# A hybrid Mamba, experts and attention kernel: the Mamba stage's B products as eight transposes, and the order of its engines laid out anew

## The reference, cut to what matters

```python
xz = hidden @ in_proj_w.T;  x, z = halves of xz          # 512 + 512 channels
u = silu(causal_conv(x, width 4) + conv_b)
dt_lo, B, C = split(u @ x_proj_w.T)                      # 64, 16, 16 columns
delta = softplus(dt_lo @ dt_proj_w.T + dt_proj_b)
A = -exp(A_log)                                          # 512 x 16
h[t] = exp(delta[t] * A) * h[t-1] + (delta[t] * u[t]) * B[t]   # per channel and state
y[t] = sum over states of h[t] * C[t]
out = ((y + u * D) * silu(z)) @ out_proj_w.T
```

## Time and profile before

| what | value |
| --- | --- |
| median of 3 runs | 3267.97 us (3264.76 to 3269.45) |
| the profiled execution: its own time | 3268.12 us |
| its span in the trace | 3266.3 us |
| share of the span busy: PE, DVE, POOL, ACT | 83%, 70%, 65%, 52% |
| first scan of the Mamba stage | starts at 58.85 us |
| last product with C of the Mamba stage | starts at 1763.12 us |
| mean granted clock of TensorE | 0.909 of full |

### The profile page before, as it was taken

The page is one execution under the profiler, slowest core; times in us unless marked ns, Lnnn a source line. Parts: engine busy times, 40 slices in busy tenths (PEclk is TensorE's granted clock), DMA queues, the critical chain, the costliest instruction groups (busy, mean ns, idle before and its releaser), DMA issues.

```text
span 3266.3 us, 55217 instructions
## 1 busy us (share of the span) xinstructions
PE 2720.5 (83%) x20862; PEld 1519.8 (47%) x20862; DVE 2293.8 (70%) x2418; ACT 1706.3 (52%) x3090; POOL 2120.7 (65%) x1317
## 2 busy tenths in 40 slices
PE   7788778887888778887855599996999999469998
PEld 3233333333344334333333355564677777445565
DVE  3999999999999999999997522212667676542211
ACT  4677777777777777777762122222444443122222
POOL 2999999999999999999995044443333333034453
PEclk9899999988999889988976599998999999679999
DMA  5556655665566565665562033432111111213442
GB/s 145 122 124 144 149 137 124 145 152 137 141 135 149 144 140 126 143 149 139 129 139 76 16 71 81 90 59 57 40 54 47 54 47 41 69 41 80 90 91 26
DMA packets 227558, 330.13 MB, mean 101 GB/s; under 512 B 40705, under 2 KB 116993, under 8 KB 227170
## 3 DMA queue, kind: packets, MB, share of 16 engines
q1 hardware_dynamic: 202722, 292.51, 36.1%
q0 software_dynamic: 24576, 34.10, 6.2%
HBM read 240.53 MB, written 85.98 MB: 100 GB/s over the span
## 4 chain that ended last, share of the span: by engine, by line
PE 44%; POOL 25%; DVE 19%; issue 6%; ACT 2%; DMA 2%; SPq 0%; DVEq 0%; POOLq 0%; ACTq 0%
POOL m_side L649 15%; PE t_wb L2230 8%; POOL m_hc L658 7%; DVE m_pair L740 7%; PE f_h L1499 7%; PE g_h L1499 7%; DVE m_hc L740 5%; PE f_yp L1513 3%; PE g_yp L1513 3%; DVE m_hc L749 2%; PE t_num L2230 2%; PE t_a_ps L2230 2%; PE m_wk L870 2%; PE m_y L967 2%; PE m_pair L1025 2%
## 5 line engine op out<-in xcount | busy, mean ns | idle before, releaser
L649 POOL TENSOR_TENSOR m_side<-m_du_r,m_bc 128x1024 f32<-128x1024 f32 x416 | 974.7, 2368 | 10.0 <-DMA m_du_r<-ddd 10.0
L394 ACT ACTIVATE m_pair<-m_delta_r,m_a_neg 128x512 f32<-128x512 f32 x832 | 539.8, 681 | 188.7 <-DVE m_hc L749 129.1
L658 POOL TENSOR_TENSOR m_hc<-m_hc,m_bc 128x1024 f32<-128x1024 f32 x208 | 492.1, 2369 | 101.7 <-DVE m_hc L740 100.0
L740 DVE TENSOR_TENSOR_SCAN m_pair<-m_pair,m_side 128x1024 f32<-128x1024 f32 x240 | 548.1, 2284 | 4.7 <-POOL m_side L649 2.5
L967 PE MATMUL m_y<-m_hc,m_fold 128*32 128x512 f32 x2048 | 320.7, 700 | 226.9 <-DVE m_hc L749 118.8
L740 DVE TENSOR_TENSOR_SCAN m_hc<-m_pair,m_side 128x1024 f32<-128x1024 f32 x176 | 397.8, 2275 | 9.8 <-ACT m_pair L394 5.6
L749 DVE TENSOR_TENSOR m_hc<-m_pair,m_bc 128x1024 f32<-128x1024 f32 x304 | 370.5, 1219 | 7.4
L870 PE MATMUL m_wk<-m_xnT,m_w_in 128*128 128x512 f32 x488 | 262.9, 665 | 0.0
L870 PE MATMUL m_wk<-m_xs,m_cw_diag 128*128 128x512 f32 x480 | 229.3, 605 | 12.8 <-ACT m_xs L461 12.8
L1025 PE MATMUL m_pair<-m_b_diag,m_du_t 128*32 128x128 f32 x6144 | 203.9, 289 | 41.2 <-DVE m_hc L740 24.2
L1025 PEld LDWEIGHTS m_pair<-m_b_diag,m_du_t 128*32 128x32 f32 x6144 | 179.0, 117 | 122.0 <-issue 120.6
(11 more groups left out here) (339 smaller groups left out, 4881.4 us busy)
## 6 DMA issues: line engine op xcount, KB each, us to landing
m_delta_r<-ddd SPq DMA_DIRECT2D x252, 256.0 KB, 6.8
m_du_r<-ddd SPq DMA_DIRECT2D x252, 256.0 KB, 7.6
m_bc<-bcd SPq DMA_DIRECT2D x256, 128.0 KB, 2.9
ddd<-m_delta SPq DMA_DIRECT2D x31, 512.0 KB, 3.1
ddd<-m_du SPq DMA_DIRECT2D x31, 512.0 KB, 4.2
f_w<-in_w SPq DMA_DIRECT2D x24, 512.0 KB, 6.0
g_w<-in_w SPq DMA_DIRECT2D x24, 512.0 KB, 6.0
m_xt<-in_x SPq DMA_DIRECT2D x16, 512.0 KB, 10.5
```

What stands on the lines that cost most here:

```text
L394: last = nc.scalar.activation(to, delta_r[:, c % 2, q, :], ACT.Exp, scale=a_neg[:, c * NQ + q, st:st + 1])
L649: nc.gpsimd.tensor_tensor(side[:, un % RING, :, :], du_r[:, c % 2, 2 * h:2 * h + 2, :], bc[:, 0, st:st + 1, :].to_broadcast([P, 2, T]), AL ...
L658: nc.gpsimd.tensor_tensor(hc[:, un % RING, :, :], hc[:, un % RING, :, :], bc[:, 1, st:st + 1, :].to_broadcast([P, 2, T]), ALU.mult).then_i ...
L740: nc.vector.tensor_tensor_scan(to, decay, added, 0.0, ALU.mult, ALU.add).then_inc(S["scan"], 1)
```

## The change

The constants (`ORDER` gives for each chunk the (set of states, half) of its eight units; before they went in the order 0, 0, 1, 1, 2, 2, 3, 3):

```diff
-ON_POOL = (0, 3, 4, 8, 9, 12, 13, 16, 18, 21, 24, 27, 28)
-ON_PE = (2, 15, 18, 22, 27, 31)
-PE_SETS = (1, 3)
+BY_PE = 3
+ORDER = (((0, 0), (0, 1), (1, 0), (1, 1), (3, 0), (2, 1), (2, 0), (3, 1)),
+         ((0, 0), (0, 1), (2, 0), (1, 1), (1, 0), (3, 1), (3, 0), (2, 1)),
+         ((0, 0), (0, 1), (1, 0), (1, 1), (2, 0), (2, 1), (3, 0), (3, 1)),
+         ((0, 0), (0, 1), (3, 0), (3, 1), (1, 0), (1, 1), (2, 0), (2, 1)))
+SET = [st for units in ORDER for st, _ in units]
+ON_POOL = (0, 2, 4, 5, 8, 9, 11, 13, 18, 20, 22, 24, 26, 28)
+ON_PE = tuple(un for un in range(UN) if SET[un] == BY_PE)
```

So `ON_PE` is now (4, 7, 13, 14, 22, 23, 26, 27): eight units, all of set 3. ACT no longer makes diagonals. It makes the product itself, on transposed data (time on the partitions, where B is one value for each partition), and PE transposes it back:

```diff
-            def diag(b, i, n):
+            def scaled(b, g, n):
...
                 for k in range(TJ):
-                    last = nc.scalar.activation(b_diag[:, i, n, k, :], ident[:], ACT.Identity,
-                                                scale=b_t[:, k, PE_SETS[i] * NL + n:PE_SETS[i] * NL + n + 1])
+                    last = nc.scalar.activation(prod[:, :, :, k, n * SB:(n + 1) * SB],
+                                                du_t[:, k, :, :].rearrange("p c (h f d) -> p (c h) f d", h=2, d=SB),
+                                                ACT.Identity, scale=b_t[:, b % 2, k, BY_PE * NL + n:BY_PE * NL + n + 1])
...
             def b_products(b, un):
...
                 for f in range(2):
-                    q = 2 * h + f
                     for k in range(TJ):
-                        for n in range(NL):
-                            last = nc.tensor.matmul(pair[n * SB:(n + 1) * SB, un % 2, f * T + k * P:f * T + (k + 1) * P],
-                                                    du_t[:, c % 2, k, q * SB:(q + 1) * SB], b_diag[:, i, n, k, :],
-                                                    start=True, stop=True, skip_group_check=True)
+                        last = nc.tensor.transpose(pair[:, un % 2, f * T + k * P:f * T + (k + 1) * P],
+                                                   prod[:, c % 2 * 2 + h, f, k, :], ident[:])
```

More of the change, by code:

```diff
@@ L55 @@
 NE_, NG_ = E_BEFORE[UN], G_BEFORE[UN]
[L56 removed]
+E_FIRST = [min(un for un in ON_PE if un // 16 == g) for g in range(2)]
+E_LAST = [E_BEFORE[16], NE_]
 G_FIRST = [min(un for un in range(8 * c, 8 * c + 8) if un not in ON_PE) for c in range(4)]
[L58 removed]
+LAST_OF = [1 + max(un for un in range(UN) if SET[un] == st) for st in range(NSET)]
+A_IX = (0, 2, 4, 5)
+A_CONV = (3, 5, 7, 10)
+A_DUT = (29, 30, 7, 12)
+A_SILU = 11
+A_XD = 12
+A_BT = 14
+A_SOFT = (13, 15, 16, 17)
+A_Z = (19, 20, 22, 27)
+A_SCALE = ((31, 32, 33, 36), (14, 18, 18, 20))
+A_NORM_OUT = (23, 24)
+A_NORM_IN = (22, 24)
+A_PT = (28, 28)
+A_SCORE = 28
+A_TR = (29, 29)
+T_IX = (0, 1, 2, 4)
+T_CONV = ((0, 0), (3, 3), (4, 5), (7, 8))
+T_DUT = (30, 30, 5, 12)
+T_OUT = (7, 10)
+T_XP = (10, 12)
+T_BT = 13
+T_DT = (12, 14, 16, 17)
+T_Z = (18, 20, 21, 25)
+T_PT = 27
+T_TR = 28
+V_GATE = (11, 17, 31, 35)
+V_RES = (9, 11)
+V_SUM_OUT = (10, 11)
+V_SUM_IN = (10, 11, 12)
+V_DELTA = (14, 15, 16, 18)
+G_OUT = 14
+G_IN = 17
+G_DU = (18, 21)
 RESET = 1e30
@@ L192, in mamba @@
                  "ab ex sp de du dz ld_c ld_l ld_p st_p pd pz xn_h "
-                 "btr b_t dut du_t dg0 dg1 dA dBu dBp scan hD hP sum yg op x1 bs1 agg1 ve1 rstd1 nm1 xn1 pt ptev scm scev").split()
+                 "btr b_t dut du_t pr dA dBu dBp scan hD hP sum yg op x1 bs1 agg1 ve1 rstd1 nm1 xn1 pt ptev scm scev").split()
         S = {n: s.sem(n) for n in names}
@@ L583, in body @@
                         nc.scalar.preload_act_table_set("natural_log_exp_and_others")
-                    if post and un in (20, 22):
-                        out_norm3(b - 1, (20, 22).index(un))
+                    if post and un in A_NORM_OUT:
+                        out_norm3(b - 1, A_NORM_OUT.index(un))
+                    if prep and un == A_XD:
+                        xd_out(b + 1)
+                    if un == A_DUT[3]:
+                        dut_out(b, 3)
+                    for n in range(NL):
+                        if un == A_SCALE[1][n]:
+                            scaled(b, 1, n)
@@ new lines, in body @@
+                        if un in A_Z:
+                            iz_out(b + 1, 1 - par, A_Z.index(un))
+                    if ahead(b) and un in A_NORM_IN:
+                        in_norm2(b + 2, A_NORM_IN.index(un))
+                    for k in range(KC):
+                        if post and un == A_PT[k]:
+                            pt_out(b - 1, k)
+                    if post and un == A_SCORE:
+                        sc_out(b - 1)
+                    for k in range(KC):
+                        if ahead(b) and un == A_TR[k]:
+                            tr_out(b + 2, k)
@@ L615, in epilogue @@
+                    for c in range(2):
+                        if prep and un == A_DUT[c]:
+                            dut_out(b + 1, c)
+                    for n in range(NL):
+                        if prep and un == A_SCALE[0][n]:
+                            scaled(b + 1, 0, n)
             def epilogue():
@@ L825, in body @@
                     scan(b, un)
-                    gates = (13, 20, 31) if prep else (13, 20, 28)
+                    if post and un + UN == V_GATE[3]:
+                        gate(b - 1, 1 - par, 3)
+                    gates = V_GATE[:3] if prep else (V_GATE[0], V_GATE[1], 28)
                     if un in gates:
@@ new lines, in body @@
+                        for dt in range(KD):
+                            for half in range(2):
+                                if un == T_CONV[dt][half]:
+                                    conv(b + 1, dt, half)
+                    if un == T_DUT[2]:
+                        dut(b, 2, post, prep)
+                    if post and un in T_OUT:
+                        outp(b - 1, T_OUT.index(un), prep)
+                    if prep and un in T_XP:
+                        xp(b + 1, 1 - par, T_XP.index(un))
@@ L1176, in body @@
+                    if post and un == T_PT:
+                        ptr(b - 1, 0, prep)
+                        ptr(b - 1, 1, prep)
+                        gate_scores(b - 1)
+                    if ahead(b) and un == T_TR:
                         tr(b + 2, 0)
                         tr(b + 2, 1)
-                    if prep and un == 29:
-                        dut(b + 1, 0, post, ahead(b))
-                        dut(b + 1, 1, post, ahead(b))
+                    for c in range(2):
+                        if prep and un == T_DUT[c]:
+                            dut(b + 1, c, post, ahead(b))
```

180 lines of the change are left out of this document (68 added, 112 removed).

## The result

| | kernel before | changed kernel |
| --- | --- | --- |
| median on the same chip | 3266.42 us (4 runs, 3264.76 to 3269.45) | 3246.3 us (4 runs, 3244.88 to 3246.65) |
| ratio of the changed kernel | | 0.9938, interval 0.9926 to 0.995 |
| span of the profiled run | 3266.3 us | 3244.8 us |
| first scan, last product with C (start) | 58.85, 1763.12 us | 59.22, 1741.55 us |

The changed kernel is faster by 20 us, 32.5 were forecast. All of the gain lies in the Mamba stage: the last product with C starts 21.6 us earlier and the span is 21.5 us shorter.

What follows compares the result with a forecast made beforehand. DVE was taken to set the pace, 97% busy. Its work (-20.0 us), fewer waits over batches 1 to 14 (-10.5) and the last batch (-2) sum to -32.5 us: 3236 us from 3268.1, range 3208 to 3280.

Steps and rivals of the forecast that it cites:

- DVE's work: On DVE, products with C go from 19 to 18 units: 1.25 us less in each of 16 batches, 20.0 us.
- PE's new price: On PE, eight transposes for a PE unit's B product take 1.1 us, where the product took 1.95.
- ACT's new price: On ACT, a `scaled` instruction of 256 columns steps 0.40 us, so a call of `scaled` takes 1.6 us.
- The waits that go: DVE's waits before `mk_delta`, at unit 2's decay and the second residual, 2.55 us a batch, should go.
- The new waits: DVE waits 1.3 us at unit 4 and 0.5 for places a walk misses, 1.8 us a batch.
- the walk: Step-by-step schedule up to unit 4: scan 4 could start at 11.8 us, PE's transposes end at 12.6, 0.8 late.
- Rival (c): PE at half clock before unit 4: scan 4 waits 4.2 to 6 us; 3282 us in all, chance 0.18.
- The sign that it named: On PE, a clock near 0.5 in the first ten microseconds of a batch would show the forecast wrong.
- the rule that speaks for (c): On PE, the Trainium skill says transposes do not count as busy for the clock; the time would be 3282 us.
- Rival (b): One wait for another: DVE's new waits sum to 3.4 to 4.3 us a batch; 3262 to 3274 us, chance 0.10.
- First and last batch: At the ends: 0 within -4 and +4 us in the first batch, -2 in the last from shorter PE products.
- the likeliest case: Whole kernel: the prediction's own forecast, 3215 to 3256 us, was given a chance of 0.60.

Runs made afterwards that it cites:

- The experiment on the B products: The changed kernel with the eight transposes of each PE unit issued as plain matmuls against the identity; measured 1.0205 of the kernel before.

## Why the prediction was right or wrong

**DVE's work: right.** The forecast was 1.25 us a batch for the product, and the run with unit 20 on DVE shows that price (3.46 for 2.20 us). Busy time fell by 1.67, though. A part of the rest is that a gate between a scan and its own product costs little: scan, gate and product take 3.91 us of the pace (801.29 to 805.20), scan and product alone 3.46 (803.43 to 806.89 in the earlier trace rows), so the gate costs 0.45 for a duration of 0.67. One more of the four gates stands there than before. This part was only read off the rows; no run isolates it. DVE's statistics of the input moved too, from units 13 to 15 to 10 to 12, which the list of places leaves out.

**PE's new price, ACT's new price: right.** Eight transposes take 1.04 us (1.1 taken), four `scaled` 1.69 us (1.6) in steps of 0.40. POOL's and ACT's sums hold as well: 771.70 / 8 = 96.5 us a batch (96.4 forecast) and 655.64 / 8 = 82.0 (82). The Trainium skill, ScalarE: Activation LUTs, What ACT_TABLE_LOAD costs, gives 186 ns and 0.833 ns a column, and about 93 ns for each operand that is one value a partition. An estimate by that page is 492 ns for 256 columns; the trace, with 496, agrees.

**The waits that go: right.** `mk_delta`, the second residual and unit 2 have none left.

**The new waits: this step failed, while the time held.** The forecast put 1.3 us at unit 4 and 0.5 for all the rest, 1.8 us a batch. Measured are 2.24 at unit 4 (31.4 us in 14 batches) and 1.07 at unit 19.

- At unit 4 the place, the order of PE's tasks and their prices were right: from `d_term`'s end to the end of the transposes the walk had 7.35 us, the trace has 7.49 (811.07 to 818.56), and scan 4 was wanted at 11.8 us and could have started at 11.82. What was mis-sized is the head of the chain: `d_term` ends at 5.9 us and not 5.2 in the best batches, and a `total` and an `ix` at the low clock make the wait a microsecond longer in 8 batches of 14. The prediction left 0.5 us for the clock.
- Rival (c) named this mechanism but costed it at 3.4 to 5 us, for a `conv` and an `ix` at the low clock. In the changed kernel only the `total` and the first `ix` behind the idle time are slow; the `conv` follows it after 0.68 us and runs in 3.70. The sign that it named, a clock near 0.5 in the first ten microseconds of a batch, didn't come: the second row of the stretches has 1.00, and the low clock lies ahead of the batch. The experiment on the B products agrees with the rule that speaks for (c), without isolating it. The time of (c), 3282, was not reached: at unit 4 the clock is worth the mean of 2.24 less the 1.42 of full clock (from the kernel with small transposes as matmuls), 0.8 us a batch, and all of DVE's waits sum to 3.3, under the 3.8 from which (c) decides.
- Rival (b) came closer: 3.3 us of waits is just under its 3.4 to 4.3. Its time was summed wrongly, too. By its own terms, -20 and 14 x 0.85 to 14 x 1.75, it is 3260 to 3273 us, or 2 less with the last batch, and not 3262 to 3274.
- At unit 19 the forecast had the decay "about 0.8 us before its scan". It named the two calls and the decay, and no wait in front of softplus of the last chunk. The `dtp` there ran at half clock behind PE's waits, and ACT idled 1.85 to 2.79 us in 13 of the 14 batches. The decay was 1.07 us late, an error of 1.9 us. With one call moved the wait goes; how much of the error is the late `dtp` no run isolates.

**First and last batch.** Up to the first table load for silu the changed kernel is 0.5 us ahead. Its first scan starts 0.4 us later, scan 2 waits 5.9 us for POOL and scan 4 3.1 us for PE, where scan 2 had waited 8.94; 0 within 4 us was forecast. The first period was 109.1 us and is 106.1, with DVE's waits in it down from 8.0 to 6.7 us. From the last of these table loads on the changed kernel wins another 5.6 us, with waits down from 5.5 to 2.0 us; -2.0 for waits and some -2 for work were forecast there.

**The sum.** Steady periods 13 x (105.98 - 105.02) = 12.5 us, first period 3.0, ahead of it 0.5, after the last 5.6, in all 21.6. The forecast had 28 us for the fourteen periods and got 15.5, and 4.5 for the ends and got 6.1. The direction, the range (3208 to 3280) and the likeliest case (3215 to 3256) held. Some luck is in it: the waits came out 1.5 us a batch above the forecast, and the 0.42 us a batch by which DVE's work fell further than priced made up for part of them. No run has the eight transposes in the old order, or the new order with the old product, so how the 20 us divide between the two isn't shown.
